# Attention scores in six banks with one maximum for two, the other products in one bank, and work moved between engines

## The chip, the cores and the metric

The kernel runs on one core of a Trainium2 chip. Its five engines run at the same time and wait for each other by semaphores: TensorE (PE in the profile; PEld are its weight loads), VectorE (DVE), ScalarE (ACT), GpSimd (POOL) and SyncE (SP), which here only issues DMAs. The metric is the time of one execution in microseconds on the device.

## The reference

Input are 8 sequences of 512 tokens with 128 features. They go through six attention layers with 16 heads of 8 features, and then through a gated feed-forward net. Cut to what matters:

```
scores = einsum('blhd,bmhd->bhlm', q, k) / sqrt(8)     # 16 heads x 512 x 512
w_avg  = softmax(scores).mean(over heads)               # 512 x 512
new_w  = softmax(w_avg + rel)                           # rel = exp(-|l-m|/16)
h1 = ln(h + new_w @ h);  h2 = ln(h1)
h  = ln(h2 + relu(h2 @ w1.T + b1) @ w2.T + b2)
```

After the six layers comes `y = x + h`, and on `ln(y)` a net with silu, gate and two gelu layers of 512, whose result is added to `y`.

## The kernel before

One sequence in one layer is a **unit**; there are 48. Its scores are cut into 64 **tiles** of 128 rows (4 heads x 32 queries) by 512 keys, numbered j = 0 to 63. A tile passes three engines: PE makes it in one of five PSUM banks (`score_tile`, L1064, four matmuls side by side in the array, each 32 columns wide), DVE takes the negative maximum of each row (`score_max`, L729), and ACT takes the exponential with that as bias and sums each row (`exp_scores`, L932). The bank is then free for the tile five further on: `score_tile` waits for that exponential. The exponentials go into a ring `ex` of 20 tiles in SBUF.

Further steps of a unit hang on these. `invert_sums` (L735) takes eight reciprocals of row sums at a time, `row_weights` on POOL (L545) spreads them over a selecting matrix, and `sum_heads` (L1082) multiplies this with four tiles of `ex`, which adds the heads up in the bank `mean` and frees the four places in the ring. ACT makes `ew` from that (`exp_mean`, L938), PE transposes it (`transpose_mean`, L1090), DVE multiplies it by a constant (`relative`, L740), PE multiplies it with the tokens (`attend`, L1071), DVE adds the residual (`residual`, L748). Normalisations follow on DVE and POOL (power -0.5 by `ALU.pow`, L517), then the layer's two products (`norm2_turn`, four `up`, four `relu` on ACT, L983, four `down`, `add`), the last normalisation, and the projection of queries and keys for the next layer (`norm3_turn`, `norm3_out`, `project`, `queries`, `keys`), split into three bf16 parts each on POOL (`split_q`, `split_k`), which go through DRAM. With six products of parts, a score has 8 x 6 = 48 rows of contraction; two heads lie in 96 rows, with zeros in `qb` for the other head.

The products outside scores and `mean` use two banks, `m0` (transposed mean and attention) and `m1` (everything else), and wait for the reader of the former content (`m0_read`, `m1_read`).

Each engine walks through slots (unit g, tile j). In a slot it first does its score step and then what the table `STEP` places there: the number of a step is its slot, counted from its unit's first, so 202 means slot 10 three units later. Parts of four units are so interleaved. An engine executes in this order and waits where its input isn't there; the slots of different engines are not tied to the same time. In steady state each unit repeats the same pattern.

After the last unit's scores come the rest of its layer and the feed-forward net (`head_...` steps, L1145 and L1168), the **tail**.

## Time and profile before

| | |
|---|---|
| time, median of 3 runs | 2652.36 us (2649.18 to 2653.47) |
| profiled execution, first to last instruction | 2651.5 us |
| PE, DVE, ACT, POOL busy | 95%, 91%, 91%, 57% |
| first exponential, end of the last | 34.15 us, 2363.6 us |
| a unit in steady state | 48.44 us |

The profiled execution has no other time of its own than its span of 2651.5 us, which lies 0.9 us under the median. The unit's 48.44 us are the distance between the first exponentials of successive units. In the views an engine's record covers an instruction from start to end; records of one engine overlap, so what an instruction costs its engine is the distance to the next start, not the record's length.

### The profile page before, as it was taken

What the parts mean: (1) busy time and instruction counts of PE and PEld (TensorE: products, weight loads), DVE (VectorE), ACT (ScalarE), POOL (GpSimd) and SP (SyncE); (2) the same over time, 40 slices, a digit from 0 to 9 for tenths busy, and PEclk for the clock granted to TensorE, in tenths of its full rate; (3) what the DMA queues carried; (4) which work ended last, traced back from release to release, by engine and by line L of the source; (5) the groups of instructions that cost most, each with busy time, mean ns of one, the idle gap of its engine ahead of it and who ended that gap; (6) DMA issues with size and microseconds to landing.
All of it is one profiled execution on the core that took longest, in us unless ns stands there. A gap on an engine that the chain in (4) does not pass through costs nothing. (4 is left out here: it accounts for less than half of the span.)

```text
span 2651.5 us, 89129 instructions
## 1 busy us (share of the span) xinstructions
PE 2528.1 (95%) x35384; PEld 1185.5 (45%) x35384; DVE 2414.4 (91%) x5440; ACT 2422.1 (91%) x6760; POOL 1516.9 (57%) x1846
## 2 busy tenths in 40 slices
PE   5999999999999999999999999999999999999999
PEld 1344444444444444444444444444444344346887
DVE  6999999999999999999999999999999999984433
ACT  5999999999999999999999999999999999983232
POOL 3568856566566565664665655656656655544211
PEclk8999999999999999999999999999999999999999
DMA  4122222211212112122112122121121221200000
GB/s 132 58 77 68 74 71 71 66 46 54 69 42 84 57 54 63 49 70 66 46 60 64 46 84 68 54 64 48 54 83 44 65 62 38 66 19 5 28 17 24
DMA packets 98913, 152.87 MB, mean 58 GB/s; under 512 B 17856, under 2 KB 81088, under 8 KB 88896
## 3 DMA queue, kind: packets, MB, share of 16 engines
q1 hardware_dynamic: 97936, 146.26, 18.4%
q8 instruction: 278, 4.55, 0.7%
q14 instruction: 139, 1.14, 0.1%
q10 hardware_dynamic: 560, 0.92, 0.1%
HBM read 92.58 MB, written 41.94 MB: 51 GB/s over the span
## 5 line engine op out<-in xcount | busy, mean ns | idle before, releaser
L932 ACT ACTIVATE ex<-sc,negmax 128x512 f32<-128x512 f32 x3072 | 2125.0, 833 | 12.8 <-DVE negmax L729 8.9
L729 DVE TENSOR_REDUCE negmax<-sc 128x1 f32<-128x512 f32 x3072 | 1922.0, 673 | 18.1 <-PE sc L1064 12.8
L1064 PE MATMUL sc<-kb,qb 96*32 96x512 bf16 x12288 | 1077.2, 385 | 85.5 <-ACT ex L932 62.5
L932 ACT ACTIVATION_READ_ACCUMULATOR ex<-sc,negmax 128x1 f32 x3072 | 1082.8, 352 | 0.0
L1082 PE MATMUL mean<-ex,rw 128*32 128x512 f32 x6144 | 796.2, 593 | 7.5 <-ACT ew L938 7.5
L1064 PEld LDWEIGHTS sc<-kb,qb 96*32 96x32 bf16 x12288 | 319.9, 94 | 1005.8 <-ACT ex L932 883.4
L545 POOL TENSOR_TENSOR rw<-sel_sb,zinv 128x256 f32<-128x256 f32 x384 | 236.4, 616 | 661.8 <-DVE zinv L735 661.5
L1082 PEld LDWEIGHTS mean<-ex,rw 128*32 128x32 f32 x6144 | 186.5, 110 | 151.9 <-issue 72.8
L1071 PE MATMUL m<-hc,pt 128*32 128x129 f32 x6144 | 206.8, 275 | 0.0
L1071 PE MATMUL m<-h2t,w_sb 128*32 128x512 f32 x1536 | 201.5, 597 | 2.4 <-ACT relu L983 2.4
L1071 PE MATMUL m<-w_sb,relu 128*32 128x128 f32 x6144 | 201.3, 273 | 0.0
L563 POOL TENSOR_TENSOR h<-h,row 128x512 f32<-128x512 f32 x144 | 185.0, 1285 | 10.9 <-POOL h L553 0.4
L1071 PEld LDWEIGHTS m<-hc,pt 128*32 128x32 f32 x6144 | 172.1, 110 | 35.4 <-DVE pt L740 25.2
L1071 PEld LDWEIGHTS m<-w_sb,relu 128*32 128x32 f32 x6144 | 169.2, 109 | 26.8 <-ACT relu L983 14.3
L983 ACT ACTIVATE relu<-m,col 128x512 f32<-128x512 f32 x192 | 168.4, 877 | 9.6 <-PE m L1071 9.6
L517 POOL TENSOR_TENSOR rstd<-veps,nhalf 128x4 f32<-128x4 f32 x160 | 163.2, 1020 | 12.5
L938 ACT ACTIVATE ew<-mean 128x512 f32<-128x512 f32 x192 | 133.3, 694 | 0.8 <-PE mean L1082 0.8
L740 DVE TENSOR_TENSOR pt<-m,g_sb 128x512 f32<-128x512 f32 x192 | 129.7, 676 | 2.4 <-PE m L1090 2.4
L1090 PE MATMUL m<-id_sb,ew 128*128 128x128 f32 x768 | 124.9, 285 | 6.5 <-DVE res L748 1.3
L1090 PEld LDWEIGHTS m<-id_sb,ew 128*128 128x128 f32 x768 | 80.6, 140 | 64.6 <-ACT ew L938 38.0
L735 DVE RECIPROCAL zinv<-zsum 128x8 f32<-128x8 f32 x384 | 73.7, 192 | 37.9 <-ACT ex L932 37.3
L553 POOL TENSOR_TENSOR h<-h,rstd 128x512 f32<-128x512 f32 x96 | 100.0, 1041 | 10.7
(124 smaller groups left out, 2425.5 us busy)
## 6 DMA issues: line engine op xcount, KB each, us to landing
kb<-qk_split SPq DMA_DIRECT2D x288, 128.0 KB
qb<-qk_split SPq DMA_DIRECT2D x568, 64.0 KB
qk_split<-kp SPq DMA_DIRECT2D x144, 128.0 KB, 1.9
qk_split<-qp SPq DMA_DIRECT2D x141, 128.0 KB, 1.8
hc<-hs SPq DMA_DIRECT2D x48, 256.0 KB, 2.8
xin<-x SPq DMA_DIRECT2D x16, 256.0 KB, 3.2
fh_raw<-fh SPq DMA_DIRECT2D x2, 1024.0 KB, 5.4
y_kept<-xin SPq DMA_DIRECT2D x8, 256.0 KB, 2.0
```

What stands on the lines that cost most here:

```text
L517: nc.gpsimd.tensor_tensor(rstd[:, k, :], veps[:, k, :], nhalf[:, :], ALU.pow).then_inc(rstd_ready[k], 1)
L545: nc.gpsimd.tensor_tensor(rw[:, c:c + ZB, :], sel_sb[:, :].rearrange("p (a q) -> p a q", a=1).to_broadcast([P, ZB, QS]), zinv[:, c:c + ZB] ...
L563: nc.gpsimd.tensor_tensor(dst, src[:, :, :], r.to_broadcast([P, NT, E]), op).then_inc(done, 1)
L729: nc.vector.tensor_reduce(negmax[:, s % RT:s % RT + 1], sc[s % NS][:, :], AX, ALU.max, negate=True) \
L740: nc.vector.tensor_tensor(pt[:, i % 2, :, :], m0[:, :].rearrange("p (c l) -> p c l", c=NT), g_sb[:, i, :, :], ALU.mult).then_inc(pt_ready, 1)
L932: nc.scalar.activation(ex[:, s % ET, :], sc[s % NS][:, :], ACT.Exp, bias=negmax[:, c:c + 1], accum_out=zsum[:, c:c + 1]).then_inc(exp_read ...
L938: nc.scalar.activation(ew[:, i % 2, :], mean[:, :], ACT.Exp).then_inc(ew_ready, 1)
L983: nc.scalar.activation(relu[:, c, :], m1[:, :], ACT.Relu, bias=col[RUN[t] % 2][:, C_B1 + c:C_B1 + c + 1]).then_inc(relu_ready, 1)
L1064: ins = nc.tensor.matmul(sc[s % NS][h * QS:h * QS + QS, :], qb[t % 2][:, h % 2, g, h // 2, r:r + QS], kb[t % 2][:, g, h // 2, :], start=Tr ...
L1071: ins = nc.tensor.matmul(dst[n * QS:n * QS + QS], lhsT[:, n * QS:n * QS + QS], rhs, start=start, stop=stop)
L1082: ins = nc.tensor.matmul(mean[n * QS:(n + 1) * QS, :], rw[:, s % RT, :], ex[:, s % ET, :], start=(g == 0), stop=(g == NG - 1))
L1090: ins = nc.tensor.transpose(m0[:, c * P:c * P + P], ew[:, i % 2, c * P:c * P + P], id_sb[:, :])
```

## The change

- The score banks become one tensor of six banks, and DVE takes the maxima of two tiles (an even one and the next) with one instruction, after both are there. PE waits for the exponential six tiles back.
- `m0` is gone: all products outside scores and `mean` go through `m1`.
- `invert_sums` moves from DVE to POOL, as a power of -1 of 8 columns.
- Relus 1 and 3 of a unit move from ACT to DVE (an addition and a maximum in one instruction).
- The contraction of a head lies in 64 rows (8 features x 8 places, two of them zero), heads in turn in the lower and upper half of the array's rows; odd tiles swap the halves. `kb` and `qb` are both filled with zeros at the start. Queries need 6 loads of 128 KB rather than 12 of 64 KB. `qb` takes half the space.
- The ring `ex` has 28 tiles, the rings of row sums 32.
- All numbers of the table `STEP` are new. Two lines stand for it in the diff.

```
...
 EPS = 1e-5
-NS = 5
-ET = 20
-RT = 24
+NS = 6
+ET = 28
+RT = 32
...
 NTERM = len(TERMS)
-ROWS = DH * NTERM
-LOADS = 3 * len(TERMS)
+SPREAD = 8
+HALF = DH * SPREAD
+LOADS = 2 * len(TERMS)
...
-    "transpose_mean": (30, 54, 68, 79),
...
-    "queries": (197,),
...
+    "transpose_mean": (36, 63, 76, 83),
...
+    "queries": (202,),
...
 }
-OLD = [(U * TILES + CH * i) % ET for i in range(2)]
+OLD = [(U * TILES + CH * i) % ET for i in range(4)]
...
 ACT_TERMS = 4
+RELU_ACT, RELU_DVE = (0, 2), (1, 3)
...
         parts.close()
-        ex = sb("ex", [P, ET, S])
...
         id_sb = sb("id_sb", [P, P])
+        minus_one = sb("minus_one", [P, ZB])
...
             return att.enter_context(nc.sbuf_tensor(name, shape, dt))
-        even_qb = att_sb("qb0", [2 * ROWS, 2, NG, 2, S], bf16)
-        kb = [att_sb(f"kb{i}", [2 * ROWS, NG, 2, S], bf16) for i in range(2)]
-        qb = [even_qb, att_sb("qb1", [2 * ROWS, 2, NG, 2, S], bf16)]
+        even_qb = att_sb("qb0", [P, NG, 2, S], bf16)
+        kb = [att_sb(f"kb{i}", [P, NG, 2, S], bf16) for i in range(2)]
+        qb = [even_qb, att_sb("qb1", [P, NG, 2, S], bf16)]
+        ex = att_sb("ex", [P, ET, S])
...
         hid_lo = [sb(f"hid_lo{i}", [P, CH, S], f32r) for i in range(2)]
+        assert OLD[2:] == [0, CH]
+        sb("ex_rest", [P, ET - 2 * CH, S])
...
         y_sb = xin
-        sc = [ctx.enter_context(nc.psum_tensor(f"sc{i}", [P, S], f32)) for i in range(NS)]
+        scores = ctx.enter_context(nc.psum_tensor("scores", [P, NS, S], f32))
+        sc = [scores[:, i, :] for i in range(NS)]
         mean = ctx.enter_context(nc.psum_tensor("mean", [P, S], f32))
-        m0 = ctx.enter_context(nc.psum_tensor("m0", [P, S], f32))
         m1 = ctx.enter_context(nc.psum_tensor("m1", [P, S], f32))
-        first_banks, value_banks, square_banks, out_banks = (sc[1], sc[2]), (sc[3], sc[4]), (sc[0], mean), (m0, m1)
+        first_banks, value_banks, square_banks, out_banks = (sc[1], sc[2]), (sc[3], sc[4]), (sc[0], mean), (sc[5], m1)
...
         KEPT = 16 * STORES
+        FILLS = 9
...
             for n, (_, ks) in enumerate(TERMS):
-                queue.dma_start(kb[t % 2][n:2 * ROWS:NTERM, :, :, :].rearrange("r g a s -> r (g a s)"),
+                queue.dma_start(kb[t % 2][n:P:SPREAD, :, :, :].rearrange("r g a s -> r (g a s)"),
...
                 qs, _ = TERMS[n]
-                for hh in range(2):
-                    queue.dma_start(qb[t % 2][ROWS * hh + n:ROWS * hh + ROWS:NTERM, hh, :, :, :].rearrange("r g a s -> r (g a s)"),
-                                    qk_dram[SEQ[t], qs, P // 2 * hh:P // 2 * hh + P // 2, :].rearrange("(r g) s -> r (g s)", g=2 * NG)) \
-                        .then_inc(qk_loaded[t % 2], 16)
...
+                queue.dma_start(qb[t % 2][n:P:SPREAD, :, :, :].rearrange("r g a s -> r (g a s)"),
+                                qk_dram[SEQ[t], qs, :, :].rearrange("(r g) s -> r (g s)", g=2 * NG)).then_inc(qk_loaded[t % 2], 16)
...
                 sp.dma_start(qk_dram[0, 3 + n, :, :], kp[n][:, :]).then_inc(kept, 16)
-            sp.wait_ge(filled, 7)
+            sp.wait_ge(filled, FILLS + 1)
...
             gp.memset(one[:, :], 1.0).then_inc(filled, 1)
+            gp.memset(minus_one[:, :], -1.0).then_inc(filled, 1)
...
             gp.memset(eps4[:, :], EPS / 4).then_inc(filled, 1)
-            gp.memset(qb[0][:, :, :, :, :].rearrange("r h g a s -> r (h g a s)").bitcast(f32), 0.0).then_inc(filled, 1)
-            gp.memset(qb[1][:, :, :, :, :].rearrange("r h g a s -> r (h g a s)").bitcast(f32), 0.0).then_inc(filled, 1)
-            gp.wait_ge(filled, 6)
+            for part in (qb[0], kb[0], qb[1], kb[1]):
+                gp.memset(part[:, :, :, :].rearrange("r g a s -> r (g a s)").bitcast(f32), 0.0).then_inc(filled, 1)
+            gp.wait_ge(filled, FILLS)
...
             gp.wait_ge(const_loaded, 32)
+            def invert_sums(t, z):
+                s = t * TILES + z * ZB
+                gp.wait_ge(exp_ready, s + ZB)
+                nc.gpsimd.tensor_tensor(zinv[:, s % RT:s % RT + ZB], zsum[:, s % RT:s % RT + ZB], minus_one[:, :], ALU.pow) \
+                    .then_inc(zinv_ready, 1)
...
             for g, j in slots:
+                for z in range(NZ):
+                    for t in due("invert_sums", z, g, j):
+                        invert_sums(t, z)
...
             def queries(n):
-                nc.vector.tensor_scalar(qf[:, :], (m0 if n < PRE else m1)[:, :], bqk_sb[LAYER_OF[n] % 2][:, 0:1], DH ** -0.5,
+                nc.vector.tensor_scalar(qf[:, :], sc[5] if n < PRE else m1[:, :], bqk_sb[LAYER_OF[n] % 2][:, 0:1], DH ** -0.5,
...
                 s = t * TILES + j
-                dve.wait_ge(scores_ready, s + 1)
-                nc.vector.tensor_reduce(negmax[:, s % RT:s % RT + 1], sc[s % NS][:, :], AX, ALU.max, negate=True) \
-                    .then_inc(max_ready, 1)
...
-            def invert_sums(t, z):
-                s = t * TILES + z * ZB
-                dve.wait_ge(exp_ready, s + ZB)
-                nc.vector.reciprocal(zinv[:, s % RT:s % RT + ZB], zsum[:, s % RT:s % RT + ZB]).then_inc(zinv_ready, 1)
+                dve.wait_ge(scores_ready, s + 2)
+                nc.vector.tensor_reduce(negmax[:, s % RT:s % RT + 2], scores[:, s % NS:s % NS + 2, :], AX, ALU.max, negate=True) \
+                    .then_inc(max_ready, 2)
...
                 wait_later(dve, sa_ready, t * NT + i - 1)
-                nc.vector.tensor_tensor(pt[:, i % 2, :, :], m0[:, :].rearrange("p (c l) -> p c l", c=NT),
+                nc.vector.tensor_tensor(pt[:, i % 2, :, :], m1[:, :].rearrange("p (c l) -> p c l", c=NT),
...
                     wait_later(dve, zz_ready, t)
-                nc.vector.scalar_tensor_tensor(res[:, i, :], hc[t % 2][:, i, :], m0[:, E:E + 1], m0[:, 0:E + 1],
+                nc.vector.scalar_tensor_tensor(res[:, i, :], hc[t % 2][:, i, :], m1[:, E:E + 1], m1[:, 0:E + 1],
...
             for g, j in slots:
-                if g < U:
-                    score_max(g, j)
-                for z in range(NZ):
-                    for t in due("invert_sums", z, g, j):
-                        invert_sums(t, z)
+                if g < U and j % 2:
+                    score_max(g, j - 1)
...
                     spread(1, t + 1)
+                for c in RELU_DVE:
+                    for t in due("relu", c, g, j):
+                        dve.wait_ge(layer_loaded[RUN[t] % 2], 64 * (RUN[t] // 2) + 64)
+                        dve.wait_ge(up_ready, t * CH + c + 1)
+                        wait_later(dve, down_ready, t * NT)
+                        nc.vector.tensor_scalar(relu[:, c, :], m1[:, :], col[RUN[t] % 2][:, C_B1 + c:C_B1 + c + 1], 0.0,
+                                                ALU.add, ALU.max).then_inc(relu_ready, 1)
...
             first_copy(1)
-            act.wait_ge(filled, 7)
+            act.wait_ge(filled, FILLS + 1)
...
                 c = s % RT
-                nc.scalar.activation(ex[:, s % ET, :], sc[s % NS][:, :], ACT.Exp, bias=negmax[:, c:c + 1],
+                nc.scalar.activation(ex[:, s % ET, :], sc[s % NS], ACT.Exp, bias=negmax[:, c:c + 1],
...
                     nc.scalar.activation(h2t[:, :], m1[:, :], ACT.Identity, bias=col[RUN[t] % 2][:, C_BB2:C_BB2 + 1]).then_inc(h2t_ready, 1)
-                for c in range(CH):
+                for c in RELU_ACT:
...
                 wait_later(pe, qf_ready, b)
-                nc.tensor.matmul(m0[:, :], wqk_sb[0][:, 0, :], h3t[:, :], start=True, stop=True).then_inc(q_ready, 1)
+                nc.tensor.matmul(sc[5], wqk_sb[0][:, 0, :], h3t[:, :], start=True, stop=True).then_inc(q_ready, 1)
...
                     pe.wait_ge(what, count)
-            def m0_read():
-                once("qf", qf_ready, PRE)
+            def m1_read():
+                assert put["down"] % NT == 0
...
-            def m1_read():
-                assert put["down"] % NT == 0
...
                 wait_later(pe, exp_ready, s - NS + 1)
-                for h in range(HG):
-                    r = i * P + n * QS
-                    ins = nc.tensor.matmul(sc[s % NS][h * QS:h * QS + QS, :], qb[t % 2][:, h % 2, g, h // 2, r:r + QS],
-                                           kb[t % 2][:, g, h // 2, :],
+                if s == NS - 1:
+                    once("qf", qf_ready, PRE)
+                r = i * P + n * QS
+                for c in range(HG):
+                    h = c ^ n % 2
+                    rows_h = slice(h % 2 * HALF, h % 2 * HALF + HALF)
+                    ins = nc.tensor.matmul(sc[s % NS][c * QS:c * QS + QS, :], qb[t % 2][rows_h, g, h // 2, r:r + QS],
+                                           kb[t % 2][rows_h, g, h // 2, :],
...
                 once("ew", ew_ready, t * NT + i + 1)
-                m0_read()
+                m1_read()
                 for c in range(NT):
-                    ins = nc.tensor.transpose(m0[:, c * P:c * P + P], ew[:, i % 2, c * P:c * P + P], id_sb[:, :])
+                    ins = nc.tensor.transpose(m1[:, c * P:c * P + P], ew[:, i % 2, c * P:c * P + P], id_sb[:, :])
...
                     pe.wait_ge(hc_loaded[t % 2], (t // 2) * 16 + 16)
-                m0_read()
+                m1_read()
                 for c in range(NT):
-                    ins = quarters(m0[:, 0:E + 1], pt[:, i % 2, c, :], hc[t % 2][:, c, :], c == 0, c == NT - 1)
+                    ins = quarters(m1[:, 0:E + 1], pt[:, i % 2, c, :], hc[t % 2][:, c, :], c == 0, c == NT - 1)
...```

How the new order differs is shown at two places of a unit, both around the projections. PE before, from the transposition of the normalised tokens `hs` (`norm3_turn`) to that of the mean `ew` (`transpose_mean`):

```order
L1020 MATMUL m1<-id_sb,hs 128x128 x4
L1064 MATMUL sc3<-kb0,qb0 32x512 x4
L1082 MATMUL mean<-ex,rw 32x512 x4
L1064 MATMUL sc4<-kb0,qb0 32x512 x4
L1064 MATMUL sc0<-kb0,qb0 32x512 x4
L1071 MATMUL m1<-h3t,wqk_sb1 32x512 x4
L1064 MATMUL sc1<-kb0,qb0 32x512 x4
L1064 MATMUL sc2<-kb0,qb0 32x512 x4
L1090 MATMUL m0<-id_sb,ew 128x128 x4
```

The same now, from the attention product ahead of it (`hc1,pt`); four matmuls on `scores` are one tile:

```order
L1085 MATMUL m1<-hc1,pt 32x129 x16
L1078 MATMUL scores<-kb0,qb0 32x512 x8
L1033 MATMUL m1<-id_sb,hs 128x128 x4
L1078 MATMUL scores<-kb0,qb0 32x512 x8
L1096 MATMUL mean<-ex,rw 32x512 x4
L1078 MATMUL scores<-kb0,qb0 32x512 x4
L1085 MATMUL m1<-h3t,wqk_sb1 32x512 x4
L1078 MATMUL scores<-kb0,qb0 32x512 x4
L1096 MATMUL mean<-ex,rw 32x512 x4
L1078 MATMUL scores<-kb0,qb0 32x512 x12
L1104 MATMUL m1<-id_sb,ew 128x128 x4
```

The transposition of the mean went to `m0` before, and goes now to the bank that the projection before it used; there are seven score tiles between the two transpositions instead of five.

DVE before, from the copy of the transposed tokens (`norm3_out`) to just behind the queries (`queries`, written to `qf`):

```order
L857 COPY h3t<-m1 128x512
L729 TENSOR_REDUCE negmax<-sc3 128x1
L748 SCALAR_TENSOR_TENSOR res<-hc1,m0 128x129
L729 TENSOR_REDUCE negmax<-sc4 128x1
L729 TENSOR_REDUCE negmax<-sc0 128x1
L735 RECIPROCAL zinv<-zsum 128x8
L729 TENSOR_REDUCE negmax<-sc1 128x1
L729 TENSOR_REDUCE negmax<-sc2 128x1
L729 TENSOR_REDUCE negmax<-sc3 128x1
L702 TENSOR_SCALAR qf<-m1,bqk_sb1 128x512
```

And now, from one product by the constant (`relative`) to the next; each maximum is of two tiles:

```order
L749 TENSOR_TENSOR pt<-m1,g_sb 128x512
L743 TENSOR_REDUCE negmax<-scores 128x2 x2
L757 SCALAR_TENSOR_TENSOR res<-hc1,m1 128x129
L743 TENSOR_REDUCE negmax<-scores 128x2
L870 COPY h3t<-m1 128x512
L743 TENSOR_REDUCE negmax<-scores 128x2 x2
L716 TENSOR_SCALAR qf<-m1,bqk_sb1 128x512
L743 TENSOR_REDUCE negmax<-scores 128x2 x2
L749 TENSOR_TENSOR pt<-m1,g_sb 128x512
```

Between the copy and the queries five single maxima became two double ones, and the reciprocals are gone from the engine.

## Rows read from the trace of the kernel before

**Rows 1.** Busy time in a steady unit and the tail (start:end, length, engines, clock)
```profile
1246.60:1295.00 48.40, 46.80 (x720) 20.34 (x712) 47.47 (x108) 48.34 (x139) 29.28 (x36) 1.00 0.19 57
2363.60:2651.50 287.90, 278.83 (x1644) 217.92 (x1644) 122.90 (x232) 93.50 (x127) 74.64 (x68) 1.00 0.06 20
```
**Rows 2.** Timeline, ACT (start, length): exponentials, then `ew`, then a relu
```profile
1287.90 0.73 ACT L932 ACTIVATE ex<-sc,negmax 128x512 f32<-128x512 f32 x1
1288.57 0.73 ACT L932 ACTIVATE ex<-sc,negmax 128x512 f32<-128x512 f32 x1
...
1246.09 0.70 ACT L938 ACTIVATE ew<-mean 128x512 f32<-128x512 f32 x1
1246.56 0.81 ACT L932 ACTIVATE ex<-sc,negmax 128x512 f32<-128x512 f32 x1
...
1271.06 0.94 ACT L983 ACTIVATE relu<-m,col 128x512 f32<-128x512 f32 x1
1271.63 0.94 ACT L932 ACTIVATE ex<-sc,negmax 128x512 f32<-128x512 f32 x1
```
**Rows 3.** Timeline, DVE, one stretch of a unit
```profile
1289.56 0.19 DVE L735 RECIPROCAL zinv<-zsum 128x8 f32<-128x8 f32 x1
1289.67 3.62 DVE L729 TENSOR_REDUCE negmax<-sc 128x1 f32<-128x512 f32 x6
1293.21 0.68 DVE L857 COPY h3t<-m 128x512 f32<-128x512 f32 x1
...
1294.41 0.34 DVE L748 SCALAR_TENSOR_TENSOR res<-hc,m 128x129 f32<-128x129 f32 x1
1294.67 0.68 DVE L729 TENSOR_REDUCE negmax<-sc 128x1 f32<-128x512 f32 x1
```
**Rows 4.** Timeline, DVE and ACT: queries, a maximum, and its exponential
```profile
1249.29 0.74 DVE L702 TENSOR_SCALAR qf<-m,bqk_sb 128x512 f32<-128x512 f32 x1
1249.94 0.68 DVE L729 TENSOR_REDUCE negmax<-sc 128x1 f32<-128x512 f32 x1
...
1250.66 0.73 ACT L932 ACTIVATE ex<-sc,negmax 128x512 f32<-128x512 f32 x1
```
**Rows 5.** Timeline: a score tile released by an exponential; a product released by DVE
```profile
1288.77 0.40 PE L1064 MATMUL sc<-kb,qb 96*32 96x512 bf16 x4 [0.27 <-ACT ex L932]
...
1200.85 0.73 DVE L702 TENSOR_SCALAR qf<-m,bqk_sb 128x512 f32<-128x512 f32 x1
1201.64 0.25 PEld L1071 LDWEIGHTS m<-h3t,wqk_sb 128*32 128x32 f32 x8 [0.41 <-DVE qf L702]
```
**Rows 6.** Timeline, PE and DVE: a score tile and its maximum
```profile
1274.49 0.39 PE L1064 MATMUL sc<-kb,qb 96*32 96x512 bf16 x4
1274.93 0.69 DVE L729 TENSOR_REDUCE negmax<-sc 128x1 f32<-128x512 f32 x1
```
**Rows 7.** Timeline, PE: projection, attention, transposition between score tiles
```profile
1249.99 0.39 PE L1064 MATMUL sc<-kb,qb 96*32 96x512 bf16 x4
1250.21 1.03 PE L1071 MATMUL m<-h3t,wqk_sb 128*32 128x512 f32 x8
1251.07 0.61 PE L1064 MATMUL sc<-kb,qb 96*32 96x512 bf16 x8
...
1257.51 1.06 PE L1071 MATMUL m<-hc,pt 128*32 128x129 f32 x32
1258.40 0.39 PE L1064 MATMUL sc<-kb,qb 96*32 96x512 bf16 x4
...
1291.52 0.40 PE L1064 MATMUL sc<-kb,qb 96*32 96x512 bf16 x4
1291.85 0.66 PE L1020 MATMUL m<-id_sb,hs 128*128 128x128 f32 x4
1292.43 0.40 PE L1064 MATMUL sc<-kb,qb 96*32 96x512 bf16 x4
```
**Rows 8.** POOL's powers of four columns (groups by line, whole run)
```profile
L517 POOL TENSOR_TENSOR rstd<-veps,nhalf 128x4 f32<-128x4 f32 x160 | 163.2, 1020 | 12.5
```

More of the change, by code:

```diff
@@ L108 @@
[L108 to L109 removed]
+    "invert_sums": (10, 19, 31, 41, 46, 53, 56, 72),
+    "row_weights": (15, 22, 38, 49, 53, 53, 61, 72),
+    "sum_heads": (21, 26, 29, 31, 39, 43, 53, 54, 58, 60, 63, 65, 71, 73, 77, 80),
+    "exp_mean": (29, 52, 65, 77),
+    "transpose_mean": (36, 63, 76, 83),
+    "relative": (36, 64, 77, 83),
+    "attend": (43, 67, 81, 87),
+    "residual": (43, 68, 81, 87),
@@ new lines @@
+    "stats0": (80, 81, 87, 89),
+    "spread": (92, 110, 183),
+    "power": (99, 112, 181),
+    "apply0": (101, 101),
+    "norm1_weight": (101,),
+    "norm1_bias": (101,),
+    "stats1": (102, 104, 105, 106),
+    "apply1": (114, 114),
+    "norm2_turn": (149,),
+    "norm2_out": (147,),
+    "token_weight": (142,),
+    "token_bias": (153,),
+    "up": (156, 161, 166, 169),
+    "relu": (153, 162, 163, 169),
+    "down": (174, 175, 178, 180),
+    "add": (179,),
+    "stats2": (182, 182, 182, 182),
@@ new lines @@
+    "apply2": (182, 185),
+    "norm3_turn": (197,),
+    "norm3_out": (197,),
+    "norm3_weight": (186,),
+    "norm3_bias": (188,),
+    "project": (200, 208),
+    "queries": (202,),
+    "keys": (205,),
+    "split_q": (215, 236, 243, 243),
+    "split_k": (230, 233, 234, 237),
+    "last_weight": (190,),
+    "last_bias": (192,),
+    "last_add": (198,),
+    "last_stats": (202,),
+    "last_spread": (207,),
+    "last_power": (210,),
+    "last_apply": (215,),
+    "last_turn": (232,),
+    "last_keep": (228,),
```

80 lines of the change are left out of this document (19 added, 61 removed).

## The prediction

> **What bounds the kernel now.** I read the busy times of one steady unit first, then the timelines of its engines. In 48.40 us ACT is busy 48.34, DVE 47.47, PE 46.80 and POOL 29.28 [rows 1]. ACT's record overlaps hide its waits, so I count its work by distances between starts: an exponential 0.66 (0.663 over a long run), an `ew` 0.47, a relu, `h2t` or `kf` 0.57 [rows 2]. A unit has 64 + 4 + 6 of them: 42.4 + 1.9 + 3.4 = 47.8 us. The unit takes 48.44, so ACT waits 0.7 us and works the rest: it is the bound. DVE is close behind: six maxima from 1289.67 to 1293.21 are 0.59 each, a copy 0.60, a residual 0.26, eight reciprocals in one 0.11, queries 0.65 [rows 3, 4]; its 47.5 busy us are nearly all work. PE has less work than its busy time says, but how late it may be is set by the ring of banks. That ring goes: an exponential starts, 0.87 later the tile for its bank starts on PE [rows 2, 5], 0.44 later its maximum [rows 6], 0.72 later its exponential [rows 4]. That is 2.0 us, and five tiles of ACT take 3.3: a slack of 1.3 us, in which a product of 0.86 (projection, also a `sum_heads`) or an attention of 0.89 on PE [rows 7] and an extra of 0.6 on DVE disappear. Attention with its layer's work is 2329 of the 2651.5 us, the tail 288, the start 34.
>
> **What the change takes away.** *Relus.* Two of four leave ACT: 2 x 0.57 = 1.14 us a unit; its work becomes 46.6. *Maxima.* A double one isn't in the trace. By the row of single ones it costs no more than 2 x 0.59 = 1.18 and no less than the 1.07 that is left if two fixed parts vanish; from the difference between 129 and 512 columns (0.26 against 0.59 to 0.65) a column costs about 1 ns, so I take 1.13, a gain of 32 x 0.055 = 1.8 us a unit on DVE. *Reciprocals.* 8 x 0.11 = 0.9 us leave DVE. *Relus on DVE.* Priced as the queries, the same kind of instruction from PSUM: 2 x 0.65 = 1.3 us come to it. DVE's work becomes 47.5 - 1.8 - 0.9 + 1.3 = 46.1. So by sums alone a unit could fall to 46.6, -1.8 us, or -83 us over the 46 units that have a layer's relus beside their scores. That is the outer end of the gain.
>
> **What it takes from the slack.** A double maximum needs both tiles, and its exponential waits for all 1024 columns. Over six tiles (3.98 us) the ring is: 0.66 to the second exponential of the pair, 0.87, 0.44, and 0.72 + 0.53 from double maximum to exponential: 3.2 us. The slack falls from 1.3 to 0.75 us. Each extra of 0.6 on DVE puts it 0.6 - 0.2 = 0.4 behind (1.33 of ACT against 1.13 for a pair), and it makes that good only by 0.2 a pair.
>
> **What the one bank costs.** Here I followed a unit through the new order by hand, from its first exponential at 0 with the full slack behind it, with a match between engines where the order gives one. ACT alone would start exponential 8 at 5.8, 10 at 7.1, 12 at 8.4. DVE: `pt` 1 waits for the transposition at PE's slot 63, so maxima (0,1) start at -1.4, (2,3) at -0.2, then the residual at 0.9. PE may turn `hs` only when `m1` is read, 0.48 after that (record 0.34 [rows 3] and 0.14 to PE): 1.37 to 1.90. Maxima (4,5) at 1.1, copy 2.3, (6,7) at 2.9. PE: scores, `sum_heads` until 3.0, then projection 3.2 to 4.06, tile 9, so maxima (8,9) at 4.5, queries 5.6 to 6.3 and maxima (10,11) only at 6.3: exponential 10 at 7.5, **0.4 late**. The next transposition of the mean, which had `m0` before, now waits for these queries, until 6.29 + 0.79 [rows 5] = 7.1, and takes 0.53; tile 13 is behind it, maxima (12,13) at 8.05, exponential 12 at 9.3: **0.85 late in all**. Going on the same way, attention 2 waits for `kf` on ACT (until 12.0) and its residual holds maxima (18,19): +0.4; attention 3 waits for `h2t`: +0.5. By slot 24 ACT has lost 1.8 us. From there to slot 42 the order gives DVE 8.6 us of work against 8.6 that ACT and the slack allow, so nothing on DVE's side, but relu 2 on ACT waits 0.3 for `up` 2, which waits for `pt` 0 to leave the bank. Slots 43 to 56 (attention, four `down`, three `sum_heads`) just fit: exponential 54 is due at 7.8 after exponential 43, its maximum allows 7.7. Sum of waits: 2.1 us, against 0.7 now.
>
> **What else moves.** POOL gets 8 powers of eight columns. Four columns take 1.02 [rows 8]; eight take between the same and twice that, 8.2 to 16.3 us a unit; with 29.3 [rows 1] it has 37.5 to 45.6 of 48.4. I take 1.4, since other work of POOL grows with its columns in part: 40.5, which hides behind ACT, with the weights for `sum_heads` 6 just in time. Without that cover it is a rival below. The larger ring `ex` takes away the wait of ACT for `sum_heads` 6, 0.3 us of the present 0.7; that is inside the count above. Loads of queries: half as many DMAs with the same bytes, an engine that nobody waits for. Zeroing covers the same bytes at the start; a DMA there less or more is within 1 us. In the tail (PE busy 278.8 of 287.9 [rows 1]) the table puts less of the net's products between the last sums and attentions, where PE now has nothing to wait for: I take +3 us for gaps there, from 0 to +9.
>
> **Sum.** 46.6 + 2.1 = 48.7 us a unit against 48.44, +0.28 x 46 = +13, and +3 in the tail: 2651.5 + 16 = 2667.5 for the profiled execution. The median stands 0.9 above it: **2668 us**. Gains and losses nearly cancel: what ACT gives away in work it takes back in waits. Break-even is at 1.8 us of waits a unit.
>
> **Rivals.**
> *The order hides more than my walk says: faster.* If the waits at the two double stops (queries, then transposition; `kf`, then attention) are 1.1 us in all rather than 1.8 by slot 24, as a few tenths of earlier starts on PE would do, and the relu's 0.3 doesn't show, a unit is 47.8: -30 us; with 0.9, as close to the sum as the present order is to its own, 47.5: -43 + 3, 2612. For it: DVE's work is 0.5 us under ACT's in the sum, and slots 24 to 56 fit to a tenth. Against it: each stop is a row's duration on a bank with one content. 2600 to 2645, chance 0.30.
> *Score tiles in half the array's rows cost PE a pause at each border: slower.* Rows show such a pause for another border. Between products of 32 columns a tile is followed after 0.22; before a transposition of 128 columns it is 0.33, and behind it 0.58 where four of 0.11 and nothing else would be 0.44 [rows 7]: some 0.1 us each way. Now every product but the scores lies in another row layout: 32 such blocks stand between score tiles in a unit's order, 64 borders, 6 us of PE. With 0.1 at each border the same walk loses about 1.4 us more in slots 43 to 56 and 8 to 16, or +64: 2730. Against it: two neighbouring tiles in other halves can now run beside each other, 0.2 us less wherever PE is behind; I had counted that. It shows as soon as a border costs over 0.02 us. Chance 0.26.
> The Trainium skill (TensorEngine Tiling (Array Packing), Key Properties) says that changing the tiling mode drains TensorE, and lists 64 rows by 32 columns as a mode apart from 128 by 32. By that rule the change comes out as this rival; the trace agrees for 128 against 32 columns, with 0.1 us, and has no tile of 64 rows.
> *POOL becomes late.* At 2 us for a power, the chain from power 0 to the weights for `sum_heads` 6 (14 us and two powers) ends two or three slots late, about 1.5 us a unit: +70, 2720. Chance 0.10.
> The forecast's own case, waits of 1.6 to 2.6 us: 2645 to 2690, chance 0.34. It lies between the others, and is what the walk gives; the pause is no row of this layout, so I don't put it in the sum.
>
> **Chances.** A measurement here tells 0.2%, 5 us, from no change. Faster by more: 0.30 from the first rival, 0.06 from my own case: 0.36. Within: 0.13, all of it my own case. Slower: 0.51, the pause, POOL and 0.15 of my own. The range for 8 in 10 is 2600 to 2735; for my own case alone 2645 to 2690.
>
> **What would show it.** Right: units of 48.4 to 49.2 us; ACT idle before exponentials 10, 12 and 18 of a unit; PE's weight loads for the transposed mean waiting for `qf`; a double maximum of 1.13 between starts. Wrong in the gain: units under 48. Wrong towards the pause: 0.3 instead of 0.22 from a tile to the next product. POOL: powers over 1.5, and `sum_heads` waiting for `rw`.

## The result, and the profile after

The changed kernel takes **2812.59 us** (median of 4 runs, 2810.4 to 2815.31) against 2652.37 beside it: ratio 1.0604, 95% interval 1.0589 to 1.0619. The forecast was 2668, with 2600 to 2735 for 8 in 10. It is 160 us slower, and lies above the stated range.

Two rows by windows answer to [rows 1]: one steady unit, from exponential 0 to the next exponential 0, and the tail (start:end, length, busy us of PE, PEld, DVE, ACT, POOL, then clock, DMA share, GB/s).
```profile
1223.80:1275.57 51.77, 47.12 (x723) 16.57 (x716) 47.86 (x70) 48.70 (x137) 42.03 (x45) 1.00 0.23 72
2512.50:2809.90 297.40, 282.22 (x1648) 220.21 (x1644) 124.96 (x235) 89.24 (x124) 84.09 (x75) 0.99 0.06 20
```
A unit takes 51.76 us (median over 41 units) where it took 48.44, the last exponential ends at 2512.5 instead of 2363.6 (+148.9), and the tail is 297.4 instead of 287.9 (+9.5). Before, ACT was busy 48.34 of 48.40; now no engine fills the unit, and the time goes into waits of the engines for each other. The total by starts of ACT's instructions, over 41 units: 46.7 us of work and 5.05 us of waits a unit, against 0.7 before. The prediction's sum had 46.6 and 2.1: ACT's work came out, the waits did not.

The costliest groups of the page (busy, mean ns of one, idle time before and its releaser):
```profile
L945 ACT ACTIVATE ex<-scores,negmax 128x512 f32<-128x512 f32 x3072 | 2076.1, 701 | 139.5 <-DVE negmax L743 131.5
L743 DVE TENSOR_REDUCE negmax<-scores 128x2 f32<-128x1024 f32 x1536 | 1860.1, 1218 | 184.5 <-PE scores L1078 154.5
L550 POOL TENSOR_TENSOR zinv<-zsum,minus_one 128x8 f32<-128x8 f32 x384 | 629.8, 1640 | 362.3 <-ACT ex L945 362.3
L1096 PE MATMUL mean<-ex,rw 128*32 128x512 f32 x6144 | 820.0, 606 | 55.2 <-POOL rw L556 52.8
```
Read the releasers as a chain: ACT waits for DVE's maxima, DVE for PE's score tiles, and PE's sums of heads for POOL's row weights, which stand as releaser in none of these rows before. A power of eight columns takes 1.64 us; I had taken 1.4.

PE's timeline shows the other half: score tiles of 64 rows between products of 128 rows (start, length).
```profile
1252.99 0.40 PE L1078 MATMUL scores<-kb,qb 64*32 64x512 bf16 x4
1253.32 1.06 PE L1096 MATMUL mean<-ex,rw 128*32 128x512 f32 x8
1254.32 0.41 PE L1078 MATMUL scores<-kb,qb 64*32 64x512 bf16 x8
1254.65 1.06 PE L1085 MATMUL m<-h2t,w_sb 128*32 128x512 f32 x8
```
From a tile to the next product are 0.33 us, where it was 0.22 [rows 7]; from a product (x8) to the next tile 1.00 instead of 0.86. Between 400 and 2000 us the medians are 0.316 against 0.216 from a tile's last matmul to the next product, and 0.52 against 0.42 from the last 512-column matmul of a product to the next tile: **a pause of 0.10 us at each border, both ways**. The scores row with x8, two tiles, also shows what the prediction had set against it: two neighbouring tiles and a border take 0.33 us, as long as one tile and a border. In [rows 7] a second tile made the row 0.22 longer (0.61 against 0.39).

Most of PE's waits are for an exponential (750.6 us in all): there PE is ahead and the ring of banks holds it. Of its other waits (us in total, times, longest) these bear on the case:
```profile
PEld mean L1096 <- POOL rw L556: 71.2, 59, 2.0
...
PEld m L1104 <- DVE qf L716: 40.7, 40, 1.4
...
PEld m L1085 <- ACT h2t L991: 37.2, 47, 1.1
...
PEld m L1085 <- ACT kf L922: 33.6, 40, 1.6
```
The last three are the stops of the one bank that the walk named (transposition behind the queries, attention behind `h2t` and `kf`), at nearly every unit. The first is POOL. Its long waits stand at one place of a unit, the ninth of its 16 sums of heads (`sum_heads` 8, slot 58 of the table): 38 of the 40 units from unit 5 on, 1.28 us each. POOL, then PE, in one of them:
```profile
1316.97 1.17 POOL L349 TENSOR_TENSOR qp<-qf,qp 128x512 bf16<-128x512 f32 x1
1318.09 1.64 POOL L550 TENSOR_TENSOR zinv<-zsum,minus_one 128x8 f32<-128x8 f32 x1
1319.69 1.19 POOL L556 TENSOR_TENSOR rw<-sel_sb,zinv 128x256 f32<-128x256 f32 x2
...
1320.36 1.07 PE L1096 MATMUL mean<-ex,rw 128*32 128x512 f32 x8 [1.29 <-POOL rw L556]
```
The table puts the power of sums 5 and the row weights 4 and 5 into the same slot, 53. POOL does the power first, so the weights that PE waits for stand behind a power that they do not need.

### The profile page after: what moved, and what is told of

The parts are those of the page before. It is cut to its first block and busy times, and to the rows that moved or that the text cites. A ratio compares the mean times of both kernels' runs of the same rounds, so it can differ in the third digit from the quotient of the medians.

```text
span 2809.9 us, 88841 instructions
## 1 busy us (share of the span) xinstructions
PE 2547.7 (91%) x35384; PEld 1012.8 (36%) x35384; DVE 2425.9 (86%) x3616; ACT 2428.4 (86%) x6662; POOL 2130.6 (76%) x2233
## 5 line engine op out<-in xcount | busy, mean ns | idle before, releaser
L945 ACT ACTIVATE ex<-scores,negmax 128x512 f32<-128x512 f32 x3072 | 2076.1, 701 | 139.5 <-DVE negmax L743 131.5
L743 DVE TENSOR_REDUCE negmax<-scores 128x2 f32<-128x1024 f32 x1536 | 1860.1, 1218 | 184.5 <-PE scores L1078 154.5
L550 POOL TENSOR_TENSOR zinv<-zsum,minus_one 128x8 f32<-128x8 f32 x384 | 629.8, 1640 | 362.3 <-ACT ex L945 362.3
L1096 PE MATMUL mean<-ex,rw 128*32 128x512 f32 x6144 | 820.0, 606 | 55.2 <-POOL rw L556 52.8
L1078 PE MATMUL scores<-kb,qb 64*32 64x512 bf16 x12288 | 759.2, 388 | 48.6 <-ACT ex L945 38.2
L945 ACT ACTIVATION_READ_ACCUMULATOR ex<-scores,negmax 128x1 f32 x3072 | 671.9, 219 | 0.0
L1078 PEld LDWEIGHTS scores<-kb,qb 64*32 64x32 bf16 x12288 | 192.9, 89 | 959.1 <-ACT ex L945 750.6
L1085 PE MATMUL m<-hc,pt 128*32 128x129 f32 x6144 | 209.9, 276 | 47.6 <-ACT h2t L991 23.2
L556 POOL TENSOR_TENSOR rw<-sel_sb,zinv 128x256 f32<-128x256 f32 x384 | 234.2, 615 | 7.8
L1085 PE MATMUL m<-h2t,w_sb 128*32 128x512 f32 x1536 | 205.0, 606 | 18.7 <-DVE pt L749 13.0
L1096 PEld LDWEIGHTS mean<-ex,rw 128*32 128x32 f32 x6144 | 121.6, 108 | 253.6 <-issue 182.4
L1085 PE MATMUL m<-w_sb,relu 128*32 128x128 f32 x6144 | 206.3, 276 | 0.0
L1085 PEld LDWEIGHTS m<-hc,pt 128*32 128x32 f32 x6144 | 160.3, 109 | 127.4 <-issue 55.7
L574 POOL TENSOR_TENSOR h<-h,row 128x512 f32<-128x512 f32 x144 | 184.2, 1279 | 11.2 <-POOL h L564 0.9
L1085 PEld LDWEIGHTS m<-w_sb,relu 128*32 128x32 f32 x6144 | 156.4, 109 | 60.5 <-issue 40.5
L522 POOL TENSOR_TENSOR rstd<-veps,nhalf 128x4 f32<-128x4 f32 x160 | 162.2, 1014 | 12.5
L1104 PE MATMUL m<-id_sb,ew 128*128 128x128 f32 x768 | 123.3, 283 | 37.8 <-DVE qf L716 21.2
L749 DVE TENSOR_TENSOR pt<-m,g_sb 128x512 f32<-128x512 f32 x192 | 130.7, 681 | 3.9 <-PE m L1104 3.9
L1104 PEld LDWEIGHTS m<-id_sb,ew 128*128 128x128 f32 x768 | 80.3, 140 | 125.3 <-issue 78.7
L951 ACT ACTIVATE ew<-mean 128x512 f32<-128x512 f32 x192 | 116.9, 609 | 1.8 <-PE mean L1096 1.8
L691 POOL TENSOR_TENSOR hid_lo<-fh_raw,hid_hi 128x512 fp32r<-128x512 f32 x12 | 15.4, 1285 | 123.5 <-DVE hid_hi L763 123.5
```

Source lines behind the costliest of these rows:

```text
L522: nc.gpsimd.tensor_tensor(rstd[:, k, :], veps[:, k, :], nhalf[:, :], ALU.pow).then_inc(rstd_ready[k], 1)
L550: nc.gpsimd.tensor_tensor(zinv[:, s % RT:s % RT + ZB], zsum[:, s % RT:s % RT + ZB], minus_one[:, :], ALU.pow) \
L556: nc.gpsimd.tensor_tensor(rw[:, c:c + ZB, :], sel_sb[:, :].rearrange("p (a q) -> p a q", a=1).to_broadcast([P, ZB, QS]), zinv[:, c:c + ZB] ...
L574: nc.gpsimd.tensor_tensor(dst, src[:, :, :], r.to_broadcast([P, NT, E]), op).then_inc(done, 1)
L743: nc.vector.tensor_reduce(negmax[:, s % RT:s % RT + 2], scores[:, s % NS:s % NS + 2, :], AX, ALU.max, negate=True) \
L749: nc.vector.tensor_tensor(pt[:, i % 2, :, :], m1[:, :].rearrange("p (c l) -> p c l", c=NT), g_sb[:, i, :, :], ALU.mult).then_inc(pt_ready, 1)
```

## The experiments

The medians of the kernel before, measured beside each group, lay between 2653.5 and 2654.7, so the groups can be compared. Waits by slot are ACT's, a unit, between exponential n and the next one: the distance of starts less ACT's work there. Three theories stood against each other. A: pauses at the borders of 64-row tiles. B: the powers on POOL. C: too little slack between double maxima and one bank.

**Taking A and B away, singly and together.** `a_rows128` lets every score product run over all 128 rows, which adds the neighbouring head's products to the scores:
```
- rows_h = slice(h % 2 * HALF, h % 2 * HALF + HALF)
+ rows_h = slice(0, P)
```


> The changed kernel (2812.6 us) with one edit: each of the four score matmuls takes all 128 rows of kb and qb instead of its head's 64. The scores of two heads are mixed by that, which leaves the number, shape and place of all instructions as they are. Theory A, the pause: each border between a tile of 64 rows and another product costs PE 0.10 us, 64 borders or 6.7 us a unit, and most of the loss comes from it; without it a unit falls from 51.8 us to 49 to 50 and the time to 2680 to 2730. Theory B, POOL: the powers of 1.64 us make the weights late and set the pace; then the time falls by 20 us at most. Theory C, slack: double maxima and the one bank set it; then it stays within 20 us, or rises, since neighbouring tiles no longer run beside each other.

`a_cheap_inverse` multiplies by a constant where the kernel inverts, so the row sums are not inverted:
```
- zsum[:, s % RT:s % RT + ZB], minus_one[:, :], ALU.pow)
+ zsum[:, s % RT:s % RT + ZB], minus_one[:, :], ALU.mult)
```


> The changed kernel with a product by a constant in place of POOL's power of -1, so that the row sums are not inverted; order and waits stay. The instruction falls from 1.64 to about 0.2 us, 11 us of POOL a unit. A (pause): POOL is late only where PE is late too, -0 to -30 us. B (POOL sets the pace): -80 us or more. C (slack): -0 to -30.

`a_rows128_cheap` has both edits.

> Both edits of the two runs before: scores from 128 rows (two heads mixed), no inversion. What is left is the order with double maxima, one bank and relus on DVE. My walk through this order gave 48.7 us a unit without any pause, and about 10 us more in the tail than before: 2675 us, range 2660 to 2700. Under C (slack worse than the walk says) it stays over 2720. If pause and POOL add up, this run's gain is the sum of the two single ones; if they cover each other, it is more than the sum.

Measured: 2797.01 (ratio 1.0537), 2791.35 (1.0516), and both together **2720.43** (1.0247, interval 1.0232 to 1.0262). Alone they give back 16 and 21 us, together 92. So each costs far more once the other is gone: the pause 71 us (2791.35 against 2720.43), the powers 77 (2797.01 against 2720.43). Two chains end at nearly the same time: with the pause gone, PE waits longer for `rw`; with the power gone, it is PE itself that comes late. In `a_rows128` the waits for `rw` grew:
```profile
PEld mean L1096 <- POOL rw L556: 127.2, 95, 2.4
```
and ACT lost 1.35 us in one place, slot 57, where in `a_cheap_inverse` nothing waited. There the operation itself became short:
```profile
L550 POOL TENSOR_TENSOR zinv<-zsum,minus_one 128x8 f32<-128x8 f32 x384 | 78.9, 206 | 586.2 <-ACT ex L945 586.1
```
With both gone, the borders are as before (tile to product, product of 8 to tile: 0.22 and 0.85), and ACT's waits are 3.16 us a unit, against 5.05. The pause's share, `a_cheap_inverse` against this one, lies in slots 41 to 53 (1.0 us) and 7 to 13 (0.4):
```profile
1307.16 0.40 PE L1078 MATMUL scores<-kb,qb 128*32 128x512 bf16 x4
1307.38 1.04 PE L1096 MATMUL mean<-ex,rw 128*32 128x512 f32 x8
1308.23 0.61 PE L1078 MATMUL scores<-kb,qb 128*32 128x512 bf16 x8
```

**C, the double maxima.** `a_single_max` is the changed kernel with one maximum for each tile, in six banks:
```
- dve.wait_ge(scores_ready, s + 2)
- nc.vector.tensor_reduce(negmax[:, s % RT:s % RT + 2], scores[:, s % NS:s % NS + 2, :], ...)
+ dve.wait_ge(scores_ready, s + 1)
+ nc.vector.tensor_reduce(negmax[:, s % RT:s % RT + 1], sc[s % NS], ...)
...
- if g < U and j % 2:
-     score_max(g, j - 1)
+ if g < U:
+     score_max(g, j)
```


> The changed kernel with one maximum for each tile as before (0.60 us each), six banks, everything else the same. DVE gets 32 x 0.06 = 2 us more work a unit, and the ring of banks gets 0.5 us more slack plus the wait for the second tile. A and B: within 25 us of 2812, in either direction, since the lateness is PE's or POOL's. C: 40 us or more faster, units under 51 us.

Measured 2925.55 (1.102): 113 us slower than with double maxima, where theory C asked for 40 faster. In this order double maxima gain. What they would cost in an order made for single ones this doesn't show: the unit grew by 2.4 us, more than the 1.6 of added work on DVE, and the largest waits stand at slots 13 (1.3) and 35 (1.2), where the changed kernel has 0.2 and 0.1. The start-to-start time of a double one is 1.14 us in the changed kernel; the sum had 1.13.

**The pause alone, in the order of before.** `b_rows64` is the kernel before with 64-row score tiles and, beside them, only what they need (`kb` and `qb` filled with zeros, six query loads rather than twelve):
```
- for h in range(HG):
-     ... sc[s % NS][h * QS:...], qb[t % 2][:, h % 2, g, h // 2, r:r + QS], kb[t % 2][:, g, h // 2, :]
+ for c in range(HG):
+     h = c ^ n % 2
+     ... sc[s % NS][c * QS:...], qb[t % 2][rows_h, g, h // 2, r:r + QS], kb[t % 2][rows_h, g, h // 2, :]
```


> The kernel before with one edit: scores of 64 rows in two halves of the partitions, with the order of heads as in the changed kernel (six terms spread over eight rows, the fill zero). Single maxima, five score banks, its own table. Theory A (every border between a tile of 64 rows and the 128-row products costs PE about 0.105 us each way, which this kernel hides only where PE has slack): 64 score tiles a unit, about 16 product groups of the heads' sums and about 20 other products between them, so PE becomes busier or paused by 2 x 0.105 us x 25 to 35 borders = 5 to 7 us a unit beside 43.7 busy; PE then fills 49 to 51 us a unit: 2652 + 55 x 1 to 2.5 us = 2700 to 2790, most likely 2720. If pauses only matter together with the changed table (their cost in the changed kernel is by lateness at slots 41 to 58): within 15 us of 2652. Rival: the halves shorten the weight loads and gain: below 2645.

Measured **2719.33** (1.0249, interval 1.0234 to 1.0264), unit 49.96 us, and the tail, which has no score tiles, 288.0 as before:
```profile
1227.79:1277.75 49.96, 48.38 (x716) 17.16 (x712) 48.06 (x108) 48.82 (x139) 29.32 (x36) 1.00 0.19 55
2429.00:2717.00 288.00, 278.85 (x1644) 217.94 (x1644) 122.83 (x232) 93.54 (x128) 74.67 (x68) 1.00 0.07 20
```
The same two borders stand in its trace. ACT's waits went from 0.7 to 2.2 us a unit, at three places: slot 9 (0.50), slot 25 (0.82), slots 43 to 47 (0.79). Scores lie in 34 blocks a unit between other products, so the pauses are 34 x 2 x 0.10 = 7 us; PE's slack and the tiles beside each other swallow 5.5 of them.

`b_rows64_ring28` adds `ET = 28` and `RT = 32` in the freed storage.

> The one before, and beside it the ring of exponentials of 28 instead of 20 tiles in the storage that the smaller query and key arrays leave. Before, the only longer wait of ScalarE is for the sums of heads that free the ring (0.32 us at slot 44). If it goes: 0.3 us x 55 units = 17 us below the 64-row version without it, and if that one costs nothing, about 2636, better than both kernels. If the wait at slot 44 only moves to the next late maximum (the slack of the ring of score banks, not of the exponentials, sets it): no difference between the two, within 5 us.

Measured 2714.11 (1.0229; the interval 1.0212 to 1.0246 overlaps that of `b_rows64`), 5 us faster where the theory had 17. The wait at slot 43 (0.50) became one at 46 (0.51): in the main the rival's outcome. The ring of exponentials was not what bound.

**The power alone, in the order of before.** `b_inverse_pool` moves the reciprocals to POOL as powers, at the slots that they had.

> The kernel before with one edit: the reciprocals as powers of -1 on GpSimd, at the same slots of its table. VectorE loses 8 x 0.11 us a unit; GpSimd gets 8 x 1.64 = 13 us a unit, and each chain exp -> inverse -> row weights -> sums of heads grows by 1.5 us at slots that leave 1 to 3 slots between (12/18, 17/20, 25/30, 36/45, 42/48, 55/56, 57/66, 66/75), which is 0.75 to 2.3 us and more. Theory B (the powers make the row weights late, PE waits, ScalarE waits for the score tiles): the place with one slot between (55/56) is late by 1 us and that with three (17/20) hardly; ScalarE loses 0.5 to 1 us a unit, 2680 to 2710. Rival (a power is hidden at any slot with more than two between, and VectorE's relief returns as much): within 10 us of 2652.

Measured 3057.03 (1.1521), 403 us slower, where I had expected 28 to 58. ACT waits 8 us a unit, 3.6 of it in one place, at slot 43, for PE's sum of heads, which frees the ring of 20 exponentials:
```profile
PEld mean L1085 <- POOL rw L553: 274.1, 173, 3.4
...
ACT ex L935 <- PE mean L1085: 181.7, 138, 3.8
```
I had counted 1.5 us on each chain. But POOL takes its instructions in order. In this table a step of a normalisation (1.04 us) and one of `split_k` (1.15) stand between the power and the row weights that PE waits for, and the power pushes all of them back. A part of the 403 us is TensorE's clock:
```profile
1210.04 1.94 PE L1085 MATMUL mean<-ex,rw 128*32 128x512 f32 x8 [2.91 <-POOL rw L553]
...
1217.10 1.06 PE L1085 MATMUL mean<-ex,rw 128*32 128x512 f32 x8 [0.39 <-ACT ew L941]
```
Behind the wait the granted clock is 0.50 (1.2 GHz) from 1210 to 1216 us, and the same product takes 1.94 us rather than 1.06. The whole run has a granted clock of 0.956, where the kernel before has 0.995: some 240 us more at the lower level. By my estimate that is at most 120 us of delay, since PE does in them what it would have done in half the time. So 403 us is not the price of the powers alone; how it divides stays open.

**One bank alone, in the order of before.** `b_one_bank` puts the transposed mean and the attention into `m1` in the kernel before and leaves `m0` unused:
```
- ins = nc.tensor.transpose(m0[:, c * P:c * P + P], ew[:, i % 2, c * P:c * P + P], id_sb[:, :])
+ ins = nc.tensor.transpose(m1[:, c * P:c * P + P], ew[:, i % 2, c * P:c * P + P], id_sb[:, :])
...
-     "attend": (40, 59, 76, 82),
+     "attend": (45, 59, 76, 82),
...
```
Three more rows of the table move beside it, as the expectation says.

> The kernel before with the transposed mean and the attention in the bank of the other products, as in the changed kernel; the freed bank stays unused, so score banks and maxima are as before. Since one bank doesn't allow the old order, the first attention moves from slot 40 to 45, the second residual from 64 to 62, the third transposition from 68 to 69 and its use on VectorE from 73 to 72. Theory C1 (the one bank is the larger part of the 66 us that remain when pauses and powers are gone: each product waits for the reader of the one before, 1.2 to 1.8 us a unit at slots 5 to 24): 2652 + 55 x 1.2 to 1.8 = 2718 to 2750. Rival C2 (the double maxima, with 0.55 us less slack, take it; the bank costs little while PE has slots to run ahead): within 20 us of 2652.

Measured 2978.95 (1.1228), 325 us slower, three times the upper bound that I gave. The first stop of the walk, in its trace:
```profile
1257.12 0.74 DVE L702 TENSOR_SCALAR qf<-m,bqk_sb 128x512 f32<-128x512 f32 x1
...
1257.91 0.42 PEld L1087 LDWEIGHTS m<-id_sb,ew 128*128 128x128 f32 x4 [2.27 <-DVE qf L702]
...
1258.95 0.69 DVE L729 TENSOR_REDUCE negmax<-sc 128x1 f32<-128x512 f32 x1 [1.09 <-PE sc L1061]
```
The transposition waits for the queries, and the score tile behind it makes DVE wait 1.09 us. The changed kernel has the same bank and, with A and B gone, lies at 2720: its new table belongs to the one bank. But the two kernels differ in more than that, so this doesn't price the bank there. The price of an edit in the old order says little of its price in an order made for it.

**Is it the transposition in the bank that still costs?** In `a_rows128_cheap_no_turn` DVE multiplies the mean itself from SBUF, and PE's transposition of it is left out:
```
- nc.vector.tensor_tensor(pt[:, i % 2, :, :], m1[:, :].rearrange(...), g_sb[:, i, :, :], ALU.mult)
+ nc.vector.tensor_tensor(pt[:, i % 2, :, :], ew[:, i % 2, :].rearrange(...), g_sb[:, i, :, :], ALU.mult)
```


> The changed kernel with scores over all 128 rows and a multiplication instead of the power (2720 us, two causes gone), and the transposition of the mean weights left out as well: VectorE multiplies the mean itself, so PE does 16 transpositions less a unit (four groups of about 0.58 us) and the one bank has four users less. It asks whether the one bank is what still costs. In that kernel ScalarE waits 3.16 us a unit, 1.84 of it at slots 7 to 23 (0.48, 0.45, 0.39, 0.13, 0.39), the places that the walk through the bank gave 1.8 us. Theory D1 (one bank): the waits at 9, 17 and 23, that stand behind transpositions and what they wait for, shrink by 0.8 to 1.2 us a unit: 2720 - 44 to 66 = 2654 to 2676. Rival D2 (the pair of maxima with too little slack, whatever the bank does): within 15 us of 2720.

Measured 2745.91 (1.0347): 25 us slower, and the waits at slots 9, 17 and 23 stayed (0.45, 0.42, 0.39). D1 is false as I put it. At slot 9 it is the queries on DVE that stand ahead of the pair of maxima, at 17 and 23 the attention on PE and its residual on DVE. That doesn't acquit the one bank, since the edit takes away only its transpositions. The attention still waits for the readers of what was in the bank before it, `h2t` and `kf`, and longer than with the transpositions (medians 1.03 and 0.74 us here, 0.28 and 0.60 there):
```profile
PE m L1084 <- ACT h2t L991: 47.4, 47, 1.0
...
PE m L1084 <- ACT kf L922: 29.7, 40, 0.7
```
The kernel before, with two banks, has neither of these waits. The new loss, at slots 41 and 63, came from the edit. DVE's product from PSUM took 678 to 695 ns in all 192 cases of `a_rows128_cheap`; from SBUF it took up to 1647, while POOL read SBUF too:
```profile
1270.63 1.60 DVE L749 TENSOR_TENSOR pt<-ew,g_sb 128x512 f32<-128x512 f32 x1
...
1269.06 2.63 POOL L574 TENSOR_TENSOR h<-h,row 128x512 f32<-128x512 f32 x2
```
The Trainium skill (SBUF — State Buffer, Who interferes with whom) says that a VectorE instruction with two SBUF inputs contends with a GpSimd instruction that reads SBUF. The trace agrees: 0.68 us at 1253.00, where POOL is idle, 1.60 beside POOL's addition.

**Relus.** `a_rows128_cheap_relus_act` gives ACT all four again (`RELU_ACT, RELU_DVE = (0, 1, 2, 3), ()`).

> The same kernel (2720 us) with all four relus on ScalarE again. ScalarE does 2 x 0.57 = 1.14 us more a unit, VectorE 1.3 less. If ScalarE's busy time sets the unit: 2720 + 55 x 1.14 = 2783. If relus on VectorE delay the pairs of maxima at slots 35 and 41 to 43 (waits there 0.05 + 0.26 + 0.33) and at 34, these waits go and the loss is 1.14 - 0.6 = 0.5 us a unit: 2748. If the relus on VectorE gave nothing (the waits take all): 2720.

Measured 2995.36 (1.1288), 275 us slower; none of my three cases. ACT's timeline, and below it PE's, at slots 34 to 36:
```profile
1443.41 0.77 ACT L996 ACTIVATE relu<-m,col 128x512 f32<-128x512 f32 x1
1443.98 0.78 ACT L945 ACTIVATE ex<-scores,negmax 128x512 f32<-128x512 f32 x1
...
1447.89 0.69 ACT L996 ACTIVATE relu<-m,col 128x512 f32<-128x512 f32 x1 [3.04 <-PE m L1085]
...
1444.32 1.09 PE L1104 MATMUL m<-id_sb,ew 128*128 128x128 f32 x4 [2.95 <-ACT relu L996]
```
Relu 1 reads the one bank later on ACT than DVE did, which runs ahead of ACT by a pair of tiles. PE's transposition waits 2.95 us for it, and relu 2 waits 3.04 us for the product behind that. A second wait of the same kind stands at slot 43, where PE's attention waits for a relu on ACT (median 1.5 us). Here too a part is TensorE's clock: behind the wait of 2.95 us it is granted 0.50 (1.2 GHz) from 1444 to 1447 us, the x8 product takes 1.62 us rather than 1.04, and the whole run has 0.960. By the same estimate that is at most some 105 of the 275 us. Even so, who empties the bank costs more here than 1.14 us of work (63 us over 55 units).

**Reciprocals back on DVE.** Three lines move from POOL's program to DVE's; `a_recip_dve` with tiles of 64 rows, `a_rows128_recip_dve` over 128.

> The changed kernel as it is (scores of 64 rows) with the reciprocals on VectorE: the move to GpSimd alone taken back. The cheap multiplication on GpSimd gave 2791 with 64 rows. Theory: the same cause is gone, so 2791 plus what VectorE's 0.9 us a unit cost, 2790 to 2810. Rival: the reciprocals on VectorE delay pairs of maxima where PE is late already, and the move had paid for itself: above 2813.

> The changed kernel with scores over all 128 rows and the true reciprocals on VectorE, as in the kernel before, at the slots of the changed table: it prices what the move to GpSimd was to save. VectorE gets 8 x 0.11 = 0.9 us a unit back, GpSimd loses 13 us of powers. Against the cheap multiplication on GpSimd (2720): if VectorE's 0.9 us lie in its idle time (it is busy 43 of 49.8 us a unit), the same within 10 us; if they fall before late pairs of maxima: up to 55 x 0.9 = 50 us more, 2770. My estimate 2735.

Measured 2873.22 (1.0827) and 2805.39 (1.0573): the first is 61 us above the changed kernel, the second 85 above `a_rows128_cheap`. One place carries it, slot 55; DVE, then ACT:
```profile
1401.94 0.20 DVE L740 RECIPROCAL zinv<-zsum 128x8 f32<-128x8 f32 x1 [1.23 <-ACT ex L944]
1402.06 2.31 DVE L734 TENSOR_REDUCE negmax<-scores 128x2 f32<-128x1024 f32 x2
...
1403.28 0.69 ACT L944 ACTIVATE ex<-scores,negmax 128x512 f32<-128x512 f32 x1 [1.37 <-DVE negmax L734]
```
The reciprocal stands at slot 56 and waits for exponential 55; the maxima for exponential 56 are queued behind it. The next two move that one number, 56 to 58, in `invert_sums`.

> The changed kernel, scores over all 128 rows, true reciprocals on VectorE, and the seventh of them at slot 58 instead of 56 (with it at 56: 2805 us, ScalarE waits 1.49 us at slot 55). Theory E1 (the place, not the move, cost): that wait goes to under 0.1 us, 1.4 x 55 = 79 us less: 2726, as with the cheap multiplication on GpSimd (2720). Rival E2 (VectorE's extra 0.9 us a unit costs wherever it stands): 2770 or more.

> The same with the scores of 64 rows: the changed kernel with its reciprocals on VectorE and one of them two slots later; it computes all that the changed kernel computes. E1: 2873 - 79 = 2794, which is 19 us below the changed kernel and as the cheap multiplication with 64 rows (2791). E2: 2840 or more.

Measured 2735.77 (1.0306) and **2804.15** (1.0564): 69 to 70 us back each time, E1. The second computes all that the changed kernel computes and is 8 us below it (intervals of the ratio 1.0546 to 1.0581 and 1.0589 to 1.0619). So the power on POOL loses a little against a well placed reciprocal, and against one at the slot of the changed table it gained 61. No version here beats the kernel before.

## Why the prediction was wrong

*ACT's work* (46.6 a unit): right, 46.7. *Double maximum* (1.13): 1.14. *Start*: first exponential at 31.8 instead of 34.2, 2 us of gain where I had said within 1. *Tail* (+3, 0 to +9): measured +9.5, just outside. It comes neither from the pause nor from the powers: +10 in `a_rows128_cheap`, none in `b_rows64`. Which of the other edits makes it I did not test.

*The walk to slot 24* (1.8 us): the sum is right, the places only in part. With A and B away ACT waits 0.48, 0.45, 0.39, 0.13 and 0.39 at slots 7, 9, 17, 19 and 23, 1.84 in all. Exponentials 10 and 18 are late as the walk says. But exponential 8, which it had on time, is late by 0.48, since PE turns `hs` at 1.60 rather than 1.37 and the projection starts at 3.68 rather than 3.2 (medians over 38 units); and exponential 12, which it had 0.45 late, loses nothing. These two errors cancel, which is luck. The relu's wait of 0.3 did not show. (Between the copy and the queries the old order has six single maxima, as its listing shows, and not the five of the sentence below it.)

*"The pause is no row of this layout, so I don't put it in the sum."* **This is the step that failed first.** A pause of 0.1 us each way stood in [rows 7] for another border, and 0.10 is what the 64-row border costs. The rival's own price for it in this order was 64 us; the measured one is 71 once the powers are gone, and it lies mostly where the rival said, in slots 41 to 53 and 7 to 13. That `b_rows64` also comes to +65 is in part chance, since that is another order with waits at other slots. I kept it out because the same rows would also let tiles run beside each other. That gain is real (two tiles in the time of one), but it stands only where two tiles follow each other, and `b_rows64`, which has gain and pause together, is 65 us slower. The Trainium skill (TensorEngine Tiling (Array Packing), Available Configurations and Key Properties) counts 64 by 32 as a tiling mode apart, and says that a change of mode drains TensorE. The traces agree in that a pause of 0.10 us stands at each border; they do not show what PE does in it.

*POOL: "which hides behind ACT, with the weights for `sum_heads` 6 just in time".* **This step failed too.** A power takes 1.64 us, not 1.4, and it doesn't hide: with the pause gone the powers cost 77 us. The late weights are those for `sum_heads` 8, not 6, behind the power in the same slot. POOL is busy 42.0 of 51.8 us, which looks like room, and still PE waits 1.28 us a unit for it. I judged cover by the sum of POOL's work and looked at the wrong place of its queue.

*Rivals taken one at a time.* Pause and powers stood at +64 and +70 as rivals of which one would hold. Both held, and there was no case for the two at once. The text gives 2720 for the second, which is 70 above the kernel before; on the forecast it is 2668 + 70 = 2738, just above the range. All three together make 2668 + 64 + 70 = 2802, near the measured 2812.6, but partly by luck: the two cost 92 together and not 134, and the rest of the sum was 52 short.

*"Slots 43 to 56 just fit".* False even without A and B: there `a_rows128_cheap` waits 0.79 us, and 0.26 at slot 41, where a statistic and relu 3 stand ahead of maxima 42 on DVE. I had no room left in the walk, and "just fits" on four queues is no fit. These waits and the tail make about the 52 us between 2668 and 2720: (3.16 - 2.1) x 46 = 49 from the waits, 7 from the tail, less 1.4 at the start.

The account of the 158 us between the two profiled spans: 89 from pauses and powers together (2809.9 against 2721.1), about 60 from the one bank, the double maxima's slack, the relus and the order (1.40 us in each of some 45 units), 10 from the tail. How the 60 divide stays open. Double maxima were undone only in the new order, the one bank was tried only in the old one, and both made the kernel far slower, each in a table made for the other case. Neither prices its part.
